# Graph attention and expert layer on one core: three instead of two of 31 gathered columns are fetched by TensorE, and ScalarE writes the segment masks

## The reference, cut to what matters

```
def _gat_conv(x, W, att_src, att_dst, bias, src, dst):
    xw = (x @ W).reshape(N, H, CPH)                      # N 6250, H 8, CPH 16
    a_s = jnp.einsum('nhc,hc->nh', xw, att_src)
    a_d = jnp.einsum('nhc,hc->nh', xw, att_dst)
    ...
    e = jax.nn.leaky_relu(a_s[src] + a_d[dst], NEG)
    m = jax.ops.segment_max(e, dst, num_segments=N)
    p = jnp.exp(e - m[dst])
    s = jax.ops.segment_sum(p, dst, num_segments=N)
    alpha = p / s[dst]
    out = jax.ops.segment_sum(xw[src] * alpha[:, :, None], dst, num_segments=N)
    return out.reshape(N, H * CPH) + bias
...
x = x + _L0_gnn_ref(_layernorm(x, axis=-1), edge_index, ...)   # two such convolutions, 206250 edges sorted by dst
x = x + _L0_ffn_ref(_layernorm(x, axis=-1)[None], ...)[0]      # top 2 of 8 experts, 256 -> 1024 -> 256
```

## Time and profile before

| | us |
|---|---|
| median of 3 runs | 3315.36 |
| lowest and highest | 3311.18, 3315.59 |
| the profiled execution | 3312.09 |
| its span, first to last instruction | 3310.3 |

### The profile page before, as it was taken

The page is one execution under the profiler, slowest core; times in us unless marked ns, Lnnn a source line. Parts: engine busy times, 40 slices in busy tenths (PEclk is TensorE's granted clock), DMA queues, the critical chain, the costliest instruction groups (busy, mean ns, idle before and its releaser), DMA issues.

```text
span 3310.3 us, 33785 instructions
## 1 busy us (share of the span) xinstructions
PE 1930.1 (58%) x8606; PEld 1397.7 (42%) x8607; DVE 2118.3 (64%) x3742; ACT 1201.3 (36%) x2081; POOL 2015.1 (61%) x2011
## 2 busy tenths in 40 slices
PE   4500000016767776776677677301345999999998
PEld 2400000003333433433343344101345999999997
DVE  8546766557887788788778878746773433333333
ACT  3313444433343334334333433412452333333332
POOL 4677777777777777777777777736663222222222
PEclk8855555558888888888888788655556999999999
DMA  9725458743344444444444444397564222222222
GB/s 290 160 56 144 151 162 154 219 150 122 122 121 143 131 122 122 153 121 121 143 131 122 121 153 122 115 230 129 157 189 145 36 36 37 37 37 36 37 35 32
DMA packets 242423, 400.68 MB, mean 121 GB/s; under 512 B 78399, under 2 KB 197843, under 8 KB 235289
## 3 DMA queue, kind: packets, MB, share of 16 engines
q1 hardware_dynamic: 163417, 247.16, 23.1%
q0 software_dynamic: 77792, 151.99, 22.4%
q10 hardware_dynamic: 1120, 0.52, 0.1%
HBM read 207.94 MB, written 191.63 MB: 121 GB/s over the span
## 4 chain that ended last, share of the span: by engine, by line
POOL 45%; PE 23%; issue 16%; DVE 7%; DMA 4%; SPq 2%; ACT 1%; DVEq 1%; POOLq 0%; ACTq 0%
POOL AR L726 43%; PE ps L1136 10%; PE ps L1142 9%; DMA out<-AR,idb 2%; POOL AR L714 1%; DVE AR L1225 1%; PE ps L1104 1%; SPq L544 1%; SPq L580 1%; POOL adstart L698 1%; ACT AR L981 1%; PE ps L1116 1%; PE ps L1033 1%; PE ps L1127 1%; PE ps L1095 1%
## 5 line engine op out<-in xcount | busy, mean ns | idle before, releaser
L726 POOL DMA_INDIRECT AR<-tables,idx x1536 | 1450.5, 944 | 468.1 <-issue 468.1
L1062 PE MATMUL ps<-AR 128*128 128x408 f32 x2584 | 976.8, 543 | 781.5 <-DVE AR L1440 781.5
L1062 PEld LDWEIGHTS ps<-AR 128*128 128x128 f32 x2584 | 526.1, 205 | 1232.0 <-issue 809.9
L806 POOL DMA_INDIRECT out<-AR,idb x105 | 195.5, 1862 | 581.6 <-issue 548.4
L1372 DVE TENSOR_TENSOR_SCAN AR<-ps,AR 128x512 f32<-128x512 f32 (+1 forms) x486 | 518.7, 1141 | 4.0
L905 ACT ACTIVATE ps<-AR 128x512 f32<-128x512 f32 x432 | 254.3, 596 | 471.1 <-DVE AR L1372 471.1
L911 ACT COPY AR<-AR 128x1984 f32<-128x1984 f32 (+1 forms) x108 | 423.2, 3966 | 0.7 <-DVE AR L1372 0.7
L1136 PEld LDWEIGHTS ps<-AR 128*128 128x128 f32 x3360 | 393.9, 193 | 6.5 <-DVE AR L1785 1.2
L1136 PE MATMUL ps<-AR 128*128 128x128 f32 x3360 | 394.5, 276 | 0.8 <-DVE AR L1785 0.8
L1366 DVE TENSOR_TENSOR AR<-AR,ps 128x3968 f32<-128x3968 f32 (+1 forms) x54 | 371.0, 6871 | 0.2
L892 ACT ACTIVATE ps<-AR 128x248 f32<-128x248 f32 (+1 forms) x54 | 20.5, 380 | 705.9 <-DVE AR L1350 705.9
(11 more groups left out here) (306 smaller groups left out, 1952.1 us busy)
## 6 DMA issues: line engine op xcount, KB each, us to landing
state<-AR SPq DMA_DIRECT2D x53, 2232.0 KB, 9.6
AR<-tables,idx POOLq DMA_INDIRECT x1585, 2.6
AR<-in_L_ffn_W SPq DMA_DIRECT2D x16, 1024.0 KB, 9.3
AR<-placed SPq DMA_DIRECT2D x105, 129.0 KB, 2.1
AR<-adstart SPq DMA_DIRECT2D x53, 248.0 KB, 4.0
adstart<-zero SPq DMA_DIRECT2D x26, 496.0 KB, 4.4
tables<-AR SPq DMA_DIRECT2D x49, 136.0 KB, 2.6
hbd<-eb2b SPq DMA_DIRECT2D x7, 896.0 KB, 9.5
```

What stands on the lines that cost most here:

```text
L726: pool.indirect_dma_start(out=G[s][:, j, 0:ROWT], out_offset=None, in_=table_rows, in_offset=bass.IndirectOffsetOnAxis(ap=idx[:, s, j:j + ...
L806: pool.indirect_dma_start(out=out, out_offset=bass.IndirectOffsetOnAxis(ap=idb[:, s, :], axis=0), in_=ys[:, s, :], in_offset=None, bounds_ ...
L1062: mm = T.matmul(ps[c][:, 0:w], onehot[c][:, a, :], table_cols[:, a * w:(a + 1) * w], start=(a == 0), stop=(a == LEV - 1))
```

## The change

PE fetches three columns instead of two, and from batch 12 on instead of 13; POOL gathers 28 columns in these 39 batches. The third column needs a place for its one-hots, its sum and its codes:

- 16 of the third column's 17 one-hots go into `eb2b` (the buffer of the biased nodes, free by then), the last one into `hT4`, as do the code differences, which were in PSUM. A copy of the level numbers goes to PSUM.
- The third sum takes bank `ps6`, so the decays have two banks, and ACT writes decay `e` when scan `e - 2` has ended instead of scan `e - 3`.
- The masks `M` and `N` of the next batch are written by ACT (`turn_marks`), between the decays and `copy_back`. DVE no longer makes them.
- POOL waits for all 117 columns before its first gather of final states, which lands in `eb2b`.

```diff
-PEC = 2
-PE0, PE1 = 13, 51
+PEC = 3
+PE0, PE1 = 12, 51
...
-        code_diff = ps[7][:, HL:HL + PEC * P].rearrange("p (c e) -> p c e", c=PEC)
+        code_diff = hT4[:, 0, P:P + PEC * P].rearrange("p (c e) -> p c e", c=PEC)
+        level_p = ps[7][:, HL:HL + LEV]
+        third_onehot = eb2b.rearrange("p e d -> p (e d)").rearrange("p (a e) -> p a e", e=P)
+        column_sum = (ps[0], ps[1], ps[6])
+
+        def level_of(c, a):
+
+            if c < 2:
+                return onehot[c][:, a, :]
+            return third_onehot[:, a, :] if a < LEV - 1 else hT4[:, 0, 0:P]
...
-            return ps[4 + e % 3][:, 0:HL if e == 0 else CH * L]
+            return ps[4 + e % 2][:, 0:HL if e == 0 else CH * L]
...
             pool.wait_ge(biased_stored, 16 * NG)
+            pool.wait_ge(columns_ready, NPC)
...
+            def turn_marks(q, n, msk):
+
+                if q >= 1:
+                    hold(act, 2, decay_diffs_ready, q)
+                S.copy(M8[:, :, 1:n + 1], bc(msk.unsqueeze(1), [P, HD, n]))
+                S.activation(N8[:, :, 1:n + 1], bc(msk.unsqueeze(1), [P, HD, n]), ACT.Identity, bias=minus_big[:, 0:1], scale=BIG).then_inc(adst_turned, 1)
...
-                    if e >= NS:
-                        hold(act, 2, entry_used, q * ENT + (e - NS + 1))
+                    if e >= 2:
+                        hold(act, 2, entry_used, q * ENT + e - 1)
...
                 batch_decays(b + 2)
+                if more:
+                    turn_marks(b + 3, J, same[:, (b + 1) * J:(b + 2) * J])
                 copy_back(b + 2, s, J)
...
-                    mm = T.matmul(ps[c][:, 0:w], onehot[c][:, a, :], table_cols[:, a * w:(a + 1) * w], start=(a == 0), stop=(a == LEV - 1))
+                    mm = T.matmul(column_sum[c][:, 0:w], level_of(c, a), table_cols[:, a * w:(a + 1) * w], start=(a == 0), stop=(a == LEV - 1))
...
                 hold(dve, 4, adst_turned, q + 1)
-                V.tensor_copy(M8[:, :, 1:n + 1], bc(msk.unsqueeze(1), [P, HD, n]))
-                dd()
-                V.tensor_scalar(N2, M2, -1.0, BIG, ALU.add, ALU.mult)
                 V.tensor_tensor_scan(E2, M2, AI2[s], 0.0, ALU.mult, ALU.add)
...
-                for c in range(PEC):
-                    V.tensor_tensor(onehot[c], bc(code_diff[:, c].unsqueeze(1), [P, LEV, P]), bc(level[:, :].unsqueeze(2), [P, LEV, P]), ALU.is_equal).then_inc(onehots_ready, 1)
+                for c in range(2):
+                    V.tensor_tensor(onehot[c], bc(code_diff[:, c].unsqueeze(1), [P, LEV, P]), bc(level_p.unsqueeze(2), [P, LEV, P]), ALU.is_equal).then_inc(onehots_ready, 1)
+                V.tensor_tensor(third_onehot, bc(code_diff[:, 2].unsqueeze(1), [P, LEV - 1, P]), bc(level_p[:, 0:LEV - 1].unsqueeze(2), [P, LEV - 1, P]), ALU.is_equal)
+                V.tensor_scalar(hT4[:, 0, 0:P], code_diff[:, 2], level_p[:, LEV - 1:LEV], None, ALU.is_equal).then_inc(onehots_ready, 1)
```

More of the change, by code:

```diff
@@ L131, in build @@
         at = XO + LEV * TPL * ROWT
-        onehot = [AR[:, at + c * LEV * P:at + (c + 1) * LEV * P].rearrange("p (a e) -> p a e", e=P) for c in range(PEC)]
-        at += PEC * LEV * P
+        onehot = [AR[:, at + c * LEV * P:at + (c + 1) * LEV * P].rearrange("p (a e) -> p a e", e=P) for c in range(2)]
+        at += 2 * LEV * P
         column_codes = AR[:, at:at + NS * PEC * P].rearrange("p (s e) -> p s e", s=NS)
@@ L183, in build @@
         level = sb("level", [P, LEV])
+        minus_big = sb("minus_big", [P, 1])
         hrow = sb("hrow", [P, 2, D])
@@ L875, in fix_exps @@
                 S.activation(fix_diff, fix_diff, ACT.Exp).then_inc(fix_exps_ready, 1)
+            def turn_marks(q, n, msk):
[3 more added lines that the diff above has]
+                S.activation(N8[:, :, 1:n + 1], bc(msk.unsqueeze(1), [P, HD, n]), ACT.Identity, bias=minus_big[:, 0:1], scale=BIG).then_inc(adst_turned, 1)
             def turn_adst(s, k, n, nth):
                 hold(act, 2, adst_loaded[s], nth)
-                S.copy(AI[s][:, :, 1:n + 1], adst_in[:, s, 0:n, k, :].rearrange("p j h -> p h j")).then_inc(adst_turned, 1)
+                S.copy(AI[s][:, :, 1:n + 1], adst_in[:, s, 0:n, k, :].rearrange("p j h -> p h j"))
             def turn_first_adst(s, k, n):
@@ L886, in turn_first_adst @@
                 S.copy(AI[s][:, :, 2:n + 1], adst_in[:, s, 1:n, k, :].rearrange("p j h -> p h j"))
-                S.copy(AI[s][:, :, 1], chunk_adst[:, k, k * HD:(k + 1) * HD]).then_inc(adst_turned, 1)
+                S.copy(AI[s][:, :, 1], chunk_adst[:, k, k * HD:(k + 1) * HD])
             def batch_weights(q, n, conv2):
@@ L923, in _ @@
             turn_first_adst(1, 1, CO[0])
+            turn_marks(0, CO[0], same1[:, 0:CO[0]])
             batch_weights(0, CO[0], True)
@@ L926, in _ @@
             batch_decays(0)
+            turn_marks(1, CO[1], same1[:, J:J + CO[1]])
             copy_back(0, 1, CO[0])
@@ L930, in _ @@
             batch_decays(1)
+            turn_marks(2, J, same[:, 0:J])
             copy_back(1, 2, CO[1])
@@ L1383, in _ @@
             V.memset(R2, -BIG)
+            V.memset(N2, -BIG)
+            V.memset(minus_big[:, :], -BIG)
+            V.tensor_copy(level_p, level[:, :])
             dd()
@@ L1423, in take_columns @@
                         n = PEC * (b - PE0) + c
-                        to, pick, of = G[b % NS][:, J - PEC + c, 0:ROWT], tile_pick[:, n, q:q + 1], ps[c][:, q * ROWT:(q + 1) * ROWT]
+                        to, pick, of = G[b % NS][:, J - PEC + c, 0:ROWT], tile_pick[:, n, q:q + 1], column_sum[c][:, q * ROWT:(q + 1) * ROWT]
                         if q == 0:
@@ L1434, in mark_columns @@
                     dve.wait_ge(x_rows_stored, 16 * NG)
+                    dve.wait_ge(biased_stored, 16 * NG)
                     V.memset(table_cols[:, NT * ROWT:LEV * TPL * ROWT], 0.0)
```

## The result

| | before | after |
|---|---|---|
| median (4 runs each) | 3314.63 | 3558.55 |
| lowest and highest | 3311.18, 3315.59 | 3557.73, 3559.18 |
| profiled execution, its span | 3312.09, 3310.3 | 3559.18, 3557.4 |

The changed kernel takes 1.0738 times as long (95% interval 1.0719 to 1.0756), some 244 us more. 3570 were forecast, with a range from 3530 to 3608: the direction, the mechanism and the size hold, and the forecast is 11 us too high.

A forecast was written before the change was run, and what follows sets the result against it. POOL's gathers bound the kernel at 36.2 us a batch; PE's burst plus DVE's hand-over would take over at 43.5. The shift of 264.9 us less 10 gave +255 on 3315.4, 3570 us, range 3530 to 3608.

The forecast's parts named there:

- main step: Edge stage: PE's burst and DVE's hand-over stand one behind the other, lengthening a batch from 36.2 to 43.5 us.
- First start: PE's first burst, batch 12: starts at 694.3 us, after batch 10's scans end at 690.72 and DVE marks batch 12.
- Third column: End of PE's burst: 17 more products, 34 records at 0.342 us, add 11.63 us at full clock.
- First two columns and the clock: PE's burst: two columns keep their 25.7 us, 2.3 of them lost at half clock after each pause.
- rival 2: PE's clock no longer falls in the shorter pauses: cycle 41.2 us, 90 us less, 3480 us; chance 0.06.
- Hand-over: DVE between PE's bursts: picks 3.07, code differences 0.62, first one-hot 2.48, in all 6.17 us.
- What was hidden: Beside PE's burst: DVE's other work leaves 10.6 us free; masks, two decay banks and POOL's slot waits cost nothing.
- Last copies: ACT's copies of batch 50 end at 2416.5 us instead of 2151.6, a shift of 264.9.
- The end of the stage: From batch 50's copies to POOL's boundary gather: 28 gathers leave the crowded stretch, 10 us less, bounds 0 and 20.
- The sum: Whole kernel: +264.9 us at the last copies, -10 at the stage's end, +255 in all.
- the first rival: POOL stays the bound and the kernel gets 51 us faster, 3264 us; chance 0.03.
- the third rival: DVE not ready when PE is, or unseen hand-over costs: 1.5 us more a batch, 57 us, 3627 us; chance 0.08.

The follow-up runs named there:

- experiment 4: Changed kernel with DVE turning columns one at a time: before the scans, after them, and at the old place, so PE always has a one-hot; 3262.69 us.
- experiment 3: Changed kernel with DVE, after the whole burst, picking column 0 and writing its next one-hot before turning to columns 1 and 2; 3464.74 us.
- experiment 2: Changed kernel with the masks written by DVE again instead of ACT; 3557.7 us.
- experiments 5 and 9: Changed kernel with POOL's first 21 final-state gathers also waiting for batch 50's copies; 4171.64 and 4171.57 us, where the kernel before took 3894.15 and 3861.71.
- experiment 8: Kernel of experiment 4 with the masks on DVE; 4235.13 us, on a chip where the kernel before took 3861.71.
- experiment 12: Kernel of experiment 4 with batch 51's store ahead of three of four `hbd` loads; 4135.81 us, where the kernel before took 3894.15.

## Why the prediction was right

Its main step, 43.5 us a batch from a burst of 37.3 and a hand-over of 6.2, held. From the first start at 695.88 to the last at 2357.63 are 38 cycles of 43.73 us. Point by point:

- **First start.** Forecast 694.3, measured 695.88. Batch 10's scans already ended 1.6 later (692.29 against the earlier trace rows), which no step had.
- **Third column.** Forecast 11.63 us; measured 11.12 + 0.85 with two overlaps of 0.16, 11.65. The earlier trace rows gave the right price for a record.
- **First two columns and the clock.** Forecast 25.7, with 2.3 lost at half clock. Measured 1015.8 / 39 = 26.05, against 23.45 without pauses (experiment 4): 2.6 lost, 0.35 a burst more than forecast. The hand-over took 0.16 of it back, which leaves the cycle's 0.2 excess. The clock kept falling, as forecast; it did so even in pauses of 4.2 us in experiment 3, so rival 2 (3480 us) is refuted for that length too. The prediction read the fall as coming about 5 us after PE fell idle, which would have left it barely inside a pause of 6.2. It comes earlier: the clock is at 0.55 in the stretch from 1.9 to 3.9 us after PE's last record here, and in experiment 3 it falls 3.5 to 4 us after it.
- **Hand-over.** Forecast 6.17, measured 5.98 between bursts. From start to start the picks took 2.90 (3.07 forecast), the differences 0.50 (0.62), the first one-hot 2.47 (2.48), and 0.11 lay between PE's last record and the first pick, which the sum had left out. The uncertain term was the code differences: 0.62 forecast, 0.42 measured as their own duration. This is the figure that the Trainium skill's rule on two elements a cycle for operands in SBUF gave (VectorE: DVE Perf Modes, section "Why PSUM operands drop a tier"). Here the trace agrees with the page: 128 elements take 0.29 us (experiment 3, line 1463) and 384 take 0.42, 0.52 ns for each more, half of the 1.09 ns that I had scaled by. The row that I had started from had its output in PSUM.
- **What was hidden.** DVE waits 11.55 us for PE (forecast 10), POOL 6.85 to 10.13 us, 8.6 on average, in 33 of its batches (forecast 8.5). The masks are worth nothing (experiment 2). ACT's decays with two banks keep their old rhythm, 0.60 us of work and 0.51 of waiting, as in the earlier trace rows:

```profile
2414.25 0.60 ACT L923 ACTIVATE ps<-AR 128x512 f32<-128x512 f32 x1 [0.51 <-DVE AR L1392]
```

- **Last copies.** Forecast 2416.5, measured 2425.6. The cycle's 0.2 us too little gives 9, the start 1.6, and the last burst (36.6 instead of 37.3) and the work behind it (31.4 instead of 31.9) take some back.
- **The end of the stage.** This is the term that the prediction sized wrongly. The prediction priced the 28 gathers by the mean share of their DMA queue, 0.37 us each, and took 10 us off, with 0 and 20 as bounds. The relief was 74.3 - 47.6 = 26.7 us, outside both. The mean was the mistake: most of the queue's gathers are of `tables`, 0.31 us each, and 21 of these 28 are of final states, 1.1 to 1.6 us each (experiments 5 and 9, and the queue's rows there).

The sum: 264.9 + 9.1 - 26.7 = 247.3 us at the boundary gather, and the spans differ by 247.1. The two errors, +9 and -17, have opposite signs by chance and leave 8 us: 3567 were forecast for the profiled execution and 3559.18 measured; with the relief sized rightly it would have been 3550, 9 us too low. The median is 11 us off, since the profiled execution lay 3.3 us under its median before and lies 0.6 over it after. The rivals: the kernel is not faster because PE's next burst can't start before the picks; experiment 4 removes just that and lands on the 3264 us that the first rival had priced. The extra links of the third rival did not appear.

## What to carry to other kernels

When work moves from a bound engine to another, add up the cycle that it joins, with the hand-over that nothing covers, and not the engine's busy share: PE stood idle for a good quarter of each batch before, and the third column still didn't fit. If the sum is over the bound, look at the hand-over before giving the change up: turning each column as soon as its successor's work is under way took 8.8 us off the batch with no instruction saved. And the cost of a transfer should be read from a stretch that holds transfers of its own kind, not from a queue's mean over the kernel, which here mixed gathers at 0.31 and at 1.6 us.

## What the runs showed of the hardware that was not expected

- On three other chips the kernel before took 3862 to 3894 us instead of 3313, and PE stood still in its one-hot products for no reason that the profile shows (653.5 us in experiment 8, none in experiment 4). In the expert stage its largest group of products kept its time (394.6 us in experiment 12, 393.5 in experiment 4). A third column means 34 more records for each batch on just the engine that stands still there: on those chips the kernels with three columns took 4136 to 4235 us, in the changed order and in that of experiment 4 alike. So the 1.5% that experiment 4 gains is shown for one chip only. On the others its order, run there only together with another edit, was slower than the kernel before.
- A gather of 128 rows of `tables` took 0.31 us of all DMA engines, one of 128 rows of final states 1.6 us with no other queue busy, and 1.3 us beside SP's reloads (27.1 us for 21), which became 23 to 28 us longer.
- PE's clock fell in pauses as short as 4.2 us. The first 68 records after such a pause (25.04 us) took 1.6 us longer than without one (23.45). The loss does not grow with the pause: 1.8 us a burst on average after 4.2 us, 2.6 after 6.0, and 2.3 after some 10.8 in the kernel before. What sets it stays open.
